# An attention stage in spans of two heads, with the output projection written into the accumulators just copied out

## The reference, cut to what matters

```python
q = (h @ wq.T).reshape(Bx, Tx, NH, HD).transpose(0, 2, 1, 3)     # NH = 4, HD = 32, Tx = 4096
k = (h @ wk.T).reshape(Bx, Tx, NKV, HD).transpose(0, 2, 1, 3)    # NKV = 2
v = (h @ wv.T).reshape(Bx, Tx, NKV, HD).transpose(0, 2, 1, 3)
...
scores = jnp.einsum('bhtd,bhsd->bhts', q, k) / jnp.sqrt(jnp.float32(HD))
scores = jnp.where(causal[None, None], scores, jnp.float32(-1e+30))
att = jax.nn.softmax(scores, axis=-1)
y = jnp.einsum('bhts,bhsd->bhtd', att, v).transpose(0, 2, 1, 3).reshape(Bx, Tx, Cx)
x = x + y @ wo.T
```

## Time and profile before

| | us |
|---|---|
| three runs, median (lowest to highest) | 7872.52 (7867.58 to 7874.14) |
| the profiled execution, its time | 7870.33 |
| the profiled execution, its span | 7868.3 |
| busy in the span: TensorE, VectorE, ScalarE | 4613.6, 5390.5, 2829.4 |
| the attention stage, from 6755 to 7303 | 548 |

### The profile page before, as it was taken

The page is one execution under the profiler, slowest core; times in us unless marked ns, Lnnn a source line. Parts: engine busy times, 40 slices in busy tenths (PEclk is TensorE's granted clock), DMA queues, the critical chain, the costliest instruction groups (busy, mean ns, idle before and its releaser), DMA issues. The chain is left out here.

```text
span 7868.3 us, 179097 instructions
## 1 busy us (share of the span) xinstructions
PE 4613.6 (59%) x57632; PEld 3119.7 (40%) x57632; DVE 5390.5 (69%) x30690; ACT 2829.4 (36%) x14714; POOL 217.7 (3%) x504
## 2 busy tenths in 40 slices
PE   4555555555555555555555555555446868788799
PEld 3444444444444444444444444444333421344344
DVE  7666666666666666666666666666646679788544
ACT  3333333333333333333333333333320010488333
POOL 0000000000000000000000000000000020000011
PEclk6555555555555555555555555555558975799799
DMA  1000000000000000000000000000004610000000
GB/s 44 14 12 14 14 12 14 14 13 14 14 14 12 14 14 13 14 14 12 14 14 12 14 14 12 14 14 12 2 2 144 200 48 0 2 1 1 24 4 5
DMA packets 93261, 164.29 MB, mean 21 GB/s; under 512 B 8711, under 2 KB 23087, under 8 KB 92337
## 3 DMA queue, kind: packets, MB, share of 16 engines
q1 hardware_dynamic: 89009, 150.47, 6.1%
q10 hardware_dynamic: 2816, 2.10, 0.1%
q0 software_dynamic: 512, 0.53, 0.0%
HBM read 146.25 MB, written 2.10 MB: 19 GB/s over the span
## 5 line engine op out<-in xcount | busy, mean ns | idle before, releaser
L431 PE MATMUL lstm_gates<-lstm_h_parts,lstm_wrec 128*128 128x1 f16 x36864 | 2074.0, 170 | 2822.8 <-DVE lstm_h_parts L576 2814.6
L431 PEld LDWEIGHTS lstm_gates<-lstm_h_parts,lstm_wrec 128*128 128x128 f16 x36864 | 1615.6, 107 | 3425.4 <-DVE lstm_h_parts L576 3414.3
L487 ACT ACTIVATE lstm_tanhs<-lstm_gates 128x3 f32<-128x3 f32 x4096 | 707.5, 173 | 2726.2 <-PE lstm_gates L431 2726.0
L431 PE MATMUL lstm_gate_o<-lstm_h_parts,lstm_wrec 128*128 128x1 f16 x12288 | 1440.7, 165 | 0.0
L576 DVE SCALAR_TENSOR_TENSOR lstm_h_parts<-lstm_tanh_o,lstm_c_pair 128x1 f16<-128x1 f32 x4096 | 645.5, 158 | 912.8 <-ACT lstm_c_pair L493 912.8
L571 DVE SCALAR_TENSOR_TENSOR lstm_terms<-lstm_tanhs 128x2 f32<-128x2 f32 x4096 | 655.1, 160 | 765.9 <-ACT lstm_tanhs L487 546.1
L595 DVE RECIPROCAL lstm_rec<-lstm_dist 128x52 f32<-128x52 f32 (+1 forms) x2560 | 1171.6, 462 | 4.2 <-issue 4.2
L493 ACT ACTIVATE lstm_c_pair<-lstm_c_pair 128x1 f32<-128x1 f32 x4096 | 639.0, 156 | 951.4 <-DVE lstm_terms L571 951.4
L431 PEld LDWEIGHTS lstm_gate_o<-lstm_h_parts,lstm_wrec 128*128 128x128 f16 x12288 | 961.2, 104 | 0.0
L454 PE MATMUL lstm_acc<-msg,lstm_wt 128*128 128x128 f32 x2048 | 780.9, 488 | 38.2 <-DVE lstm_wt L603 38.2
L582 DVE TENSOR_TENSOR lstm_h_parts<-hid_t,lstm_h_parts 128x1 f16<-128x1 f32 x4096 | 667.5, 163 | 179.9 <-DVE hid_t L578 13.1
(11 more groups left out here) (260 smaller groups left out, 4626.0 us busy)
## 6 DMA issues: line engine op xcount, KB each, us to landing
lstm_ring<-in_adj SPq DMA_DIRECT2D x256, 256.0 KB, 2.7
gnn_ring<-in_adj SPq DMA_DIRECT2D x64, 1024.0 KB, 5.2
w<-in_w SPq DMA_DIRECT2D x2, 1364.0 KB, 9.5
heads_cos<-in_cos SPq DMA_DIRECT2D x8, 256.0 KB, 3.1
heads_sin<-in_sin SPq DMA_DIRECT2D x8, 256.0 KB, 3.5
qs<-heads_q_high SPq DMA_DIRECT2D x64, 32.0 KB, 2.3
out<-x SPq DMA_DIRECT2D x8, 256.0 KB, 2.3
ks<-heads_k_high ACTq DMA_DIRECT2D x16, 64.0 KB, 2.6
```

The lines of the kernel that those rows point to most:

```text
L431: return nc.tensor.matmul(o, wrec[:, w, g, :], h_parts[:, (n - 1) % NH, k:k + 1], start=False, stop=True, skip_group_check=True)
L487: nc.scalar.activation(tanhs[:, 0:3], gates[t % 2][:, i, :], ACT.Tanh, scale=unscale).then_inc(tanhs_ready, 1)
```

## The change

The four heads of a group are no longer gone through together. A *span* is a group and one key/value head, so two heads; there are 16 spans of 4 to 32 units, and spans of heads 0 and 1 alternate with spans of heads 2 and 3. Each span has two accumulators of its own, and those of the other pair of heads stay untouched. The accumulators become whole banks of 128 partitions. At the end of a span ScalarE copies its two accumulators; the projection of that span then goes into the same two banks (`pair_out`), two tiles at a time (a *round*): the two heads of one tile to one bank. Round 0 is issued on TensorE ahead of the sixth unit's score of the next span, round 1 four units later (two later for span 0) and after the additions of round 0. VectorE takes round 0 behind the fourth unit and round 1 three units later (two for span 0). The multiplication that starts a span waits until all tiles of the span before the last are added. The wait ahead of scores for the additions, and that of the projections for empty score tiles, are gone. A tile is now added to the residual in two parts, each with a reciprocal of two sums and two additions.

```diff
--- before.py
+++ after.py
@@ -1134,14 +1134,16 @@
     BEHIND = 4
     with Phase(nc, "attend") as ph:
         sc = [ph.ps(f"sc{i}", [P, 2, G]) for i in range(2)]
-        heads = [ph.ps(f"heads{h}", [VW, G]) for h in range(NHEAD)]
+        banks = [ph.ps(f"heads{h}", [P, G]) for h in range(NHEAD)]
+        heads = [bank[0:VW, :] for bank in banks]
+        pair_out = [bank[:, 0:2 * (P + 1)] for bank in banks]
 
         exp32 = [T.xn_t[:, i * 2 * G:(i + 1) * 2 * G].rearrange("p (k q) -> p k q", k=2) for i in range(NB)]
         high = [ph.sb(f"high{i}", [P, 2, G], F16) for i in range(NB)]
         low = [ph.sb(f"low{i}", [P, 2, G], F16) for i in range(NB)]
         ot = ph.sb("ot", [VW, NHEAD, G])
         wo = ph.sb("wo", [VW, NHEAD, P + 1])
-        inv = ph.sb("inv", [P, 2, NHEAD])
+        inv = ph.sb("inv", [P, 2, 2])
         loaded, wo_zeroed, wo_one = ph.sem("loaded"), ph.sem("wo_zeroed"), ph.sem("wo_one")
         scored, exps_ready, multiplied = ph.sem("scored"), ph.sem("exps_ready"), ph.sem("multiplied")
         high_ready, low_ready = ph.sem("high_ready"), ph.sem("low_ready")
@@ -1149,8 +1151,11 @@
         inv_ready, head_added, added = ph.sem("inv_ready"), ph.sem("head_added"), ph.sem("added")
         block = ph.block()
 
-        units = [(g, 2 * pair, h) for g in range(NG) for pair in range(2 * (g + 1)) for h in range(NHEAD)]
-        first_of = [units.index((g, 0, 0)) for g in range(NG)] + [len(units)]
+        units = [(g, 2 * pair, h) for g in range(NG) for kv in range(NKV) for pair in range(2 * (g + 1))
+                 for h in (2 * kv, 2 * kv + 1)]
+        first_of = [units.index((g, 0, 2 * kv)) for g in range(NG) for kv in range(NKV)] + [len(units)]
+        NSPAN = NKV * NG
+        ROUND = 2
 
         def queries(u):
 
@@ -1159,9 +1164,17 @@
 
         def after(u, n):
 
-            for g in range(NG - 1):
-                if u == first_of[g + 1] + n:
-                    return g
+            for span in range(NSPAN - 1):
+                if u == first_of[span + 1] + n:
+                    return span
+            return None
+
+        def round_at(u, n, late):
+
+            for i in range(ROUND):
+                for span in range(NSPAN - 1):
+                    if u == first_of[span + 1] + n + i * (2 if span == 0 else late):
+                        return span, i
             return None
 
         @block.sync
@@ -1192,8 +1205,8 @@
             def multiply(u):
                 g, tile, h = units[u]
                 c = queries(u)
-                if u == first_of[g] and g >= 1:
-                    pe.wait_ge(heads_out, NHEAD * g)
+                if u in first_of and g >= 1:
+                    pe.wait_ge(added, TPG * (first_of.index(u) - 1))
                 pe.wait_ge(low_ready, u + 1)
                 for k in range(2):
                     values = T.v_parts[:, tile + k, h // 2, :]
@@ -1203,48 +1216,46 @@
                                                 stop=True, skip_group_check=True)
                 last.then_inc(multiplied, 1)
 
-            def project(g, k):
-                if g * TPG + k >= 2:
-                    pe.wait_ge(added, g * TPG + k - 1)
-                for h in range(NHEAD):
-                    o = sc[k % 2][:, h // 2, (h % 2) * (P + 1):(h % 2 + 1) * (P + 1)]
-                    last = nc.tensor.matmul(o, ot[:, h, k * P:(k + 1) * P], wo[:, h, :], start=True, stop=True)
-                last.then_inc(projected, 1)
+            def project(span, i):
+
+                g, kv = divmod(span, NKV)
+                pe.wait_ge(heads_out, 2 * (span + 1))
+                if i:
+                    pe.wait_ge(added, TPG * span + i * (TPG // ROUND))
+                for b in range(TPG // ROUND):
+                    k = i * (TPG // ROUND) + b
+                    for h in range(2):
+                        o = pair_out[2 * kv + b][:, h * (P + 1):(h + 1) * (P + 1)]
+                        last = nc.tensor.matmul(o, ot[:, 2 * kv + h, k * P:(k + 1) * P], wo[:, 2 * kv + h, :],
+                                                start=True, stop=True)
+                    last.then_inc(projected, 1)
 
             pe.wait_ge(loaded, 3 * 16)
             pe.wait_ge(wo_one, 1)
             for u in range(len(units)):
-                for k in range(TPG):
-                    g = after(u, BEHIND + 2 + k // 2 * 2)
-                    if g is not None:
-                        if k % 2 == 0:
-                            pe.wait_ge(heads_out, NHEAD * (g + 1))
-                            pe.wait_ge(exps_ready, u)
-                        project(g, k)
-                for k in range(TPG):
-                    g = after(u, BEHIND + 2 + k)
-                    if g is not None:
-                        pe.wait_ge(added, TPG * g + k + 1)
+                due = round_at(u, BEHIND + 1, 4)
+                if due is not None:
+                    project(*due)
                 score(u)
                 if u >= BEHIND:
                     multiply(u - BEHIND)
             for u in range(len(units) - BEHIND, len(units)):
                 multiply(u)
-            pe.wait_ge(heads_out, NHEAD * NG)
-            for k in range(TPG):
-                project(NG - 1, k)
+            for i in range(ROUND):
+                project(NSPAN - 1, i)
 
         @block.scalar
         def _(act):
             unit = act.alloc_register("score_unit")
             act.reg_load(unit, T.score_unit[0:1, 0:1].bitcast(I32))
 
-            def heads_away(g):
-                act.wait_ge(multiplied, first_of[g + 1])
-                if g >= 1:
-                    act.wait_ge(projected, TPG * g)
-                for h in range(NHEAD):
-                    nc.scalar.copy(ot[:, h, :], heads[h][:, :]).then_inc(heads_out, 1)
+            def heads_away(span):
+                kv = span % NKV
+                act.wait_ge(multiplied, first_of[span + 1])
+                if span >= NKV:
+                    act.wait_ge(projected, TPG * (span - 1))
+                for h in (2 * kv, 2 * kv + 1):
+                    nc.scalar.copy(ot[:, h, :], heads[h][0:VW, :]).then_inc(heads_out, 1)
 
             for u in range(len(units)):
                 c = queries(u)
@@ -1259,10 +1270,10 @@
                     exp = nc.scalar.activation(high[u % NB][:, :, c], sc[u % 2][:, :, c], ACT.Exp, bias=PROB_SHIFT,
                                                scale=unit)
                 exp.then_inc(exps_ready, 1)
-                g = after(u, BEHIND - 1)
-                if g is not None:
-                    heads_away(g)
-            heads_away(NG - 1)
+                span = after(u, BEHIND - 1)
+                if span is not None:
+                    heads_away(span)
+            heads_away(NSPAN - 1)
 
         @block.gpsimd
         def _(pool):
@@ -1273,24 +1284,25 @@
         @block.vector
         def _(dve):
 
-            def add_tile(g, k):
-
-                t = TPG * g + k
-                dve.wait_ge(projected, t + 1)
-                s2 = sc[k % 2][:, :, 0:2 * (P + 1)].rearrange("p a (b c) -> p a b c", b=2)
-                if t >= 2:
-                    dve.wait_ge(added, t - 1)
-                nc.vector.reciprocal(inv[:, k % 2, :].rearrange("p (a b) -> p a b", a=2),
-                                     s2[:, :, :, P]).then_inc(inv_ready, 1)
-                dve.wait_ge(inv_ready, t + 1)
-                for h in range(NHEAD):
-                    ins = nc.vector.scalar_tensor_tensor(out=T.xn[:, t, :], in0=s2[:, h // 2, h % 2, 0:P],
-                                                         scalar=inv[:, k % 2, h:h + 1], in1=T.xn[:, t, :],
-                                                         op0=ALU.mult, op1=ALU.add)
-                    if h < NHEAD - 1:
-                        ins.then_inc(head_added, 1)
-                        dve.wait_ge(head_added, (NHEAD - 1) * t + h + 1)
-                ins.then_inc(added, 1)
+            def add_round(span, i):
+
+                g, kv = divmod(span, NKV)
+                for b in range(TPG // ROUND):
+                    k = i * (TPG // ROUND) + b
+                    n, t = TPG * span + k, TPG * g + k
+                    both = pair_out[2 * kv + b].rearrange("p (h c) -> p h c", h=2)
+                    dve.wait_ge(projected, n + 1)
+                    if n >= 2:
+                        dve.wait_ge(added, n - 1)
+                    nc.vector.reciprocal(inv[:, n % 2, :], both[:, :, P]).then_inc(inv_ready, 1)
+                    dve.wait_ge(inv_ready, n + 1)
+                    if kv:
+                        dve.wait_ge(added, n - TPG + 1)
+                    nc.vector.scalar_tensor_tensor(out=T.xn[:, t, :], in0=both[:, 0, 0:P], scalar=inv[:, n % 2, 0:1],
+                                                   in1=T.xn[:, t, :], op0=ALU.mult, op1=ALU.add).then_inc(head_added, 1)
+                    dve.wait_ge(head_added, n + 1)
+                    nc.vector.scalar_tensor_tensor(out=T.xn[:, t, :], in0=both[:, 1, 0:P], scalar=inv[:, n % 2, 1:2],
```

(13 more changed lines are left out.)

## The result

| | before | changed |
|---|---|---|
| median of six runs each, us | 7870.85 (7865.7 to 7874.14) | 7797.48 (7795.31 to 7800.7) |
| profiled execution, time / span, us | 7870.33 / 7868.3 | 7795.31 / 7793.5 |
| attention stage, first cast to end of the last addition, us | 543.9 | 473.0 |

The ratio of the times is 0.9907 (95% interval 0.9895 to 0.992), 73.4 us by the medians.

A forecast was written before the change was run, and what follows sets the result against it. VectorE was taken to set the attention stage's pace except at seams; 467.0 + 7.0 + 0.4 + 4.1 = 478.5 us against 543.9, 65.4 us less, gave a median of 7807 us, range 7798 to 7833.

The forecast's parts named there:

- What bounds the stage: Attention stage: VectorE sets the pace, a pair of units every 3.00 us, except at seams, which hold 71.7 us of waits.
- Added on VectorE: Additions to the residual: 64 tiles of 0.93 us replace 32 of 1.64 us, 7.0 us more.
- the bare durations: Lower bound for a new tile on VectorE: 0.18 + 2 x 0.35 = 0.88 us, giving 3.8 us more.
- Removed: the wait for the copies: Seams: TensorE's first multiplication no longer waits for accumulator copies (3.14 us idle before), only for additions, late only at span 2.
- Moved: the projections: Seams: first projected tile ready at 5.1 us, wanted by VectorE at 6.0, so the seams' 71.7 us go to nothing.
- Start and span 2: First spans: VectorE waits about 1 us for a projection and 0.4 for an exponential; 0.4 us more than before.
- The end: End of the stage: waits of 2.9 us for the first round and 1.1-1.2 for the second, together 4.1 us.
- the floor of 467 us: Attention stage: 543.9 us less 76.9 us of VectorE's waits leaves 467.0 us, the least before added work.
- From the profile to the median: Whole kernel: the median of the runs, 7872.52 us, was taken as 2.2 us above the profiled execution's time.
- The clock: Rival at seams: TensorE's idles lower its clock, 15 to 43 us back, about 7828 us; chance 0.20.
- Seams did not stall: Rival: every seam stalls as before, 15 x 10.2 = 153 us, 7960 us; decides from 4.4 us per seam; chance 0.04.
- no effect: Rival: added seams and reciprocals cost the gain, time within 0.2% (16 us), a seam of 3.3 to 5.4 us; chance 0.03.

The follow-up runs named there:

- e1: The changed kernel, with VectorE made to wait for the second addition of each tile before going on: 7804.02 us.
- e4: The changed kernel with a second, unused reciprocal in each of the 64 tiles: 7800.43 us.
- e5: The changed kernel with each round of two tiles done by one reciprocal of four sums and four interleaved additions: 7784.57 us.
- e6: The changed kernel with VectorE's first round queued behind the third unit of the next span, not the fourth: 7803.04 us.
- e8: The changed kernel run again, unchanged, to compare the stretches around the stage: one execution, 7792.45 us, stage 471.1 us.
- e2: The changed kernel with projections back in the score tiles, ahead of the seventh and ninth unit's score, and scores waiting for the additions: 7880.25 us.
- e3: The kernel before, with VectorE's additions behind its fifth and seventh unit of the next group, not the third and fifth: 7848.89 us.

## Why the prediction was wrong

It was wrong by its range. The stage was forecast 65.4 us shorter and is 70.9 us shorter. Point by point:

- *What bounds the stage.* Right. VectorE's pairs still start every 3.00 us away from seams, and e1, e4, e5 and e6 show that time added to or taken from VectorE appears in the stage nearly in full (6.1 of 7.4 us, 4.1 of 4.2, 12.4 of 14.6, 3.5 of 4.4).
- *Added on VectorE: the step that failed.* "A new tile is 0.21 + 2 x 0.36 = 0.93 us" took the mean over the four additions of an old tile. They are not alike. Where the next addition waits for the result, the step is 7129.05 - 7128.67 = 0.38 to 0.39 us; behind the last, for which nothing waits, the next instruction starts 7129.32 - 7129.05 = 0.27 us later. The old tile has three steps of the first kind and one of the second, 0.20 + 3 x 0.39 + 0.27 = 1.64; the new one has one of each: 0.20 + 0.38 + 0.27 = 0.85. The rows before held both: four additions last 1.51 us from the first start to the last end and one lasts 0.35, so three steps are 1.51 - 0.35 = 1.16, or 0.39 each, and 1.43 - 1.16 = 0.27 is left for the last. The 64 tiles take 54.9 us, not 59.5, and the old 32 took 53.1, not 52.5: 1.8 us more where 7.0 were forecast, 5.2 us of the miss. The lower bound failed with it: "the bare durations", 0.88, are no bound, since instructions start before the one ahead has ended. The Trainium skill, "Perfetto Trace Analysis", section "Optimizing Scalar/DVE Operations", says that the write-acknowledgement half of an instruction's profiled latency overlaps with the next instruction; the rows show such an overlap where nothing waits for the result, 0.08 us of an addition's 0.35 (0.27 apart) and 0.08 of a reciprocal's 0.16 (e4), and none where something does. e1 removes the cheap step and pays 7.4 us in tiles; e5 makes more steps cheap and gets 8.2 us by it.
- *Removed: the wait for the copies.* Right, no such wait at any later seam; TensorE waited once for additions, ahead of span 2, as said (1.3 us, 2.0 forecast).
- *Moved: the projections.* Right, number by number, at the last seam: copies done at 4.5 us (4.35 forecast), TensorE idle 1.32 (1.6), projection at 4.56 (4.4), VectorE at 6.0 (6.0), second projection at 10.8 (10.6), VectorE there at 12.6 (12.7). e6 puts the first tile at 5.3 (5.1).
- *Start and span 2.* 3.25 us of idle where the old start's 1.6 and 0.4 more were forecast: 1.2 us too little. Of it, the 1.12 us that the cast at 6763.87 waited for a multiplication were not in the walk; they fell away in one repeat (e8). *The end.* 3.9 us, 4.1 forecast. The casts and subtractions themselves, which the floor of 467 us took as given, are 1.3 us less (543.89 and 472.95 us less tiles and idle give 412.28 and 410.94). So the miss in the stage is 5.2 - 1.0 + 1.3 = 5.5 us. That the last two terms nearly cancel, and the miss looks like that of the tile alone, is chance.
- *From the profile to the median.* The median came out 9.5 us below the forecast, so some 4 us of the miss lie outside the stage, where the forecast had put nothing. In the two profiles the stretches around the stage are 1.1 and 2.7 us shorter. As the repeats show, scatter is enough for the 1.1; for the 2.7 it stays open. Counted by medians, 1.7 of the 4 us are the starting point: "the median of the runs, 7872.52" was of three, and six gave 7870.85.
- *The rivals.* The clock did not take anything back: 1.00 from 6764 to 7227, with an idle of 1.3 us ahead of the projection at eleven seams. Seams did not stall. e2 shows that both rivals were real ones and come together: with the projection left in the score tiles TensorE idles 2.28 us, the clock falls, and the seams cost 5.7 us each (86 / 15), above the 4.4 from which stalling decides. That there was no effect is out: 73.4 us are well beyond the 16 us of that rival.
- *The range.* Its low end, 7798, was the forecast less 9 us, of which only 3 were a bound from rows, and that bound was wrong. With the tile priced as measured, the same sum gives about 7807 - 5 = 7802.

## What to carry to other kernels

On an engine that sets the pace, cost a short dependent sequence step by step, each by start to start and with what waits for it; a mean over the sequence does not carry to a shorter one, and durations are no lower bound. When an engine idles at a seam, ask which buffer the late work needs: here accumulators for two spans without the new place of the projection gained nothing (e2), and later additions alone gained 21 us (e3); with the projection in banks that had just come free it was 73. That place without the split into spans was not run. Then order what is left so that no instruction waits for the one just ahead of it.

## What the runs showed of the hardware that was not expected

A wait for the instruction just ahead costs VectorE about 0.12 us per 128 x 128 float32 addition: 0.39 us from start to start with it, 0.27 without, at a duration of 0.35 us either way. For a reciprocal of 128 x 2 the steps are 0.20 us, to an addition that waits for it, and 0.08 us, to a second reciprocal that does not, at a duration of 0.16.

TensorE's granted clock stayed at 1.00 across eleven seams with an idle of 1.3 us in each (changed kernel). At a seam with an idle of 2.28 us (e2) it was 0.55 over 15 us, and at one with 3.14 us (the kernel before) 0.69 over 22 us.
